# A transformer block on one core: a new order of the first batches, with 16 products whose result nobody reads

## The reference

```python
ada = silu(c) @ W_ada + b_ada            # c: 32 x 288, one row for each batch
shift_msa, scale_msa, gate_msa, shift_mlp, scale_mlp, gate_mlp = split(ada, 6)
h = layernorm(x) * (1 + scale_msa) + shift_msa
x = x + gate_msa * attention(h, W_qkv, b_qkv, W_proj, b_proj)
h = layernorm(x) * (1 + scale_mlp) + shift_mlp
x = x + gate_mlp * (gelu(h @ W_fc1 + b_fc1) @ W_fc2 + b_fc2)
```

## Time and profile before

| | |
|---|---|
| median of 3 runs | 1203.75 us |
| the profiled execution | 1203.89 us, of which the span is 1202.1 us |
| TensorE busy | 1158.4 us (96%), mean granted clock 0.984 |
| VectorE, ScalarE, GpSimd busy | 77%, 71%, 48% |

### The profile page before, as it was taken

The page is one execution under the profiler, slowest core; times in us unless marked ns, Lnnn a source line. Parts: engine busy times, 40 slices in busy tenths (PEclk is TensorE's granted clock), DMA queues, the critical chain, the costliest instruction groups (busy, mean ns, idle before and its releaser), DMA issues.

```text
span 1202.1 us, 28774 instructions
## 1 busy us (share of the span) xinstructions
PE 1158.4 (96%) x10375; PEld 993.9 (83%) x10375; DVE 920.6 (77%) x1928; ACT 858.0 (71%) x1485; POOL 579.2 (48%) x619
## 2 busy tenths in 40 slices
PE   6888999999999999999999999999999999999987
PEld 5666788888888888888888888888888888888777
DVE  5578878878878788887778888877888887877553
ACT  4378777777777777777777787777777777778721
POOL 3012444555544445554454555445455544544664
PEclk9779999999999999999999999999999999999999
DMA  9454554455555445555544555555445555444220
GB/s 276 137 172 156 163 164 147 150 175 168 164 159 163 149 148 173 166 171 164 163 151 151 159 179 165 165 159 167 143 149 181 164 165 161 158 148 156 83 68 20
DMA packets 133814, 186.93 MB, mean 156 GB/s; under 512 B 24284, under 2 KB 102150, under 8 KB 133675
## 3 DMA queue, kind: packets, MB, share of 16 engines
q1 hardware_dynamic: 133513, 184.66, 48.9%
q10 hardware_dynamic: 162, 0.44, 0.1%
HBM read 119.92 MB, written 64.60 MB: 153 GB/s over the span
## 4 chain that ended last, share of the span: by engine, by line
PE 92%; DVE 3%; ACT 2%; DMA 1%; issue 1%; SPq 0%; POOL 0%; ACTq 0%; POOLq 0%; DVEq 0%
PE a_bank L855 13%; PE x_bank L768 12%; PE turn_bank L822 10%; PE b_bank L855 9%; PE score_bank L793 7%; PE st_bank L810 7%; PE b_bank L869 7%; PE b_bank L870 6%; PE b_bank L871 6%; PE a_bank L836 5%; PE x_bank L776 5%; PE x_bank L742 2%; PE a_bank L742 1%; ACT e L942 1%; PE x_bank L745 1%
## 5 line engine op out<-in xcount | busy, mean ns | idle before, releaser
L1128 DVE TENSOR_REDUCE mx<-score_bank 128x2 f32<-128x512 f32 x512 | 332.3, 685 | 94.6 <-PE score_bank L793 92.8
L942 ACT ACTIVATE e<-st_bank 128x1024 f32<-128x1024 f32 x256 | 262.3, 1024 | 163.9 <-PE st_bank L810 163.3
L1285 POOL TENSOR_TENSOR gl<-gl_raw,gh 128x512 fp32r<-128x512 f32 (+1 forms) x160 | 197.2, 1241 | 180.8 <-DVE gh L1193 180.8
L935 ACT CAST ql<-mxt 4x256 fp32r<-4x256 f32 x512 | 205.7, 402 | 5.3
L869 PE MATMUL b_bank<-w,gh 128*128 128x288 f32 x576 | 179.1, 311 | 2.0 <-DVE tmp L1199 1.9
L870 PE MATMUL b_bank<-w,gh 128*128 128x288 f32 x576 | 170.6, 296 | 0.0
L871 PE MATMUL b_bank<-w,gl 128*128 128x288 f32 x576 | 169.6, 295 | 0.0
L822 PE MATMUL turn_bank<-e,ve 128*32 128x256 f32 x2048 | 125.8, 387 | 0.1
L810 PE MATMUL st_bank<-ql,kl 58*128 58x256 f32 x1024 | 117.9, 309 | 6.1 <-ACT e L942 5.0
L793 PE MATMUL score_bank<-kl,ql 58*128 58x256 f32 x1024 | 120.7, 314 | 2.7 <-DVE mx L1128 1.9
L855 PE MATMUL a_bank<-xh,w 128*128 128x256 f32 x640 | 112.2, 298 | 5.5 <-DVE xr L1107 4.0
(11 more groups left out here) (152 smaller groups left out, 2490.9 us busy)
## 6 DMA issues: line engine op xcount, KB each, us to landing
qk_rows<-qst SPq DMA_DIRECT2D x128, 256.0 KB, 3.7
ql<-qk_rows SPq DMA_DIRECT2D x384, 72.0 KB
kl<-qk_rows SPq DMA_DIRECT2D x378, 72.0 KB
o_rows<-on SPq DMA_DIRECT2D x128, 128.0 KB
gate<-gates SPq DMA_DIRECT2D x32, 432.0 KB, 4.5
xin<-in_x SPq DMA_DIRECT2D x32, 288.0 KB, 4.1
x<-in_x SPq DMA_DIRECT2D x32, 288.0 KB, 4.0
out<-x SPq DMA_DIRECT2D x32, 288.0 KB, 2.2
```

What stands on the lines that cost most here:

```text
L935: last = nc.scalar.copy(rows[:, :, :, a, :], src)
L942: nc.scalar.activation(e[:, j % 4, :, :, :].rearrange("p i u l -> p (i u l)"), st_bank[:, :, :, :].rearrange("p i u l -> p (i u l)"), ACT. ...
L1128: nc.vector.tensor_reduce(mx[:, j // HP, i, :, col:col + 1], score_bank[i][:, :].rearrange("p (t l) -> p t l", t=NT), AX.X, ALU.max).then_ ...
L1285: nc.gpsimd.tensor_tensor(gl[:, cols], g[:, cols], gh[:, cols].bitcast(F32), ALU.subtract).then_inc(g_lo, 1)
```

## The change

1. SyncE issues loads 3 to 6 only ahead of its list; 7 to 11 become steps of the list (`("load", 0, 7)` and so on).
2. The second half of the modulation is cut into ten pieces, `("mod", 0, 0)` to `("mod", 0, 9)`, spread over the list. Pieces 0, 1, 5 and 6 have 128 columns of weights and three products each; the other six have 32 columns and three products each.
3. The scores of batches 0 and 1 are made head by head (`s_head`, "sh"): head h waits for the maximum of head h-2 alone.
4. The remainders of loads 3, 4, 6, 7, 9, 10 and 11 are taken by GpSimd (`split_late`) in place of VectorE; loads 5 and 8 stay with VectorE.
5. Twelve steps `("warm", 0, n)` issue n products each, 16 in all, of 128 x 128 weights with 512 columns moving, into `turn_bank`, which nobody reads before it is written anew.
6. The five heads are in a new order; the repeating order and the tails are as before.

```diff
 PE_HEAD = [
-    ("xt", 0, 0), ("xt", 0, 1), ("qk", 0, 0), ("qk", 0, 1), ("qk", 0, 2), ("gate2", 0, 0), ("v", 0, 0), ("v", 0, 1),
-    ("xt", 1, 0), ("mod", 0, 0), ("xt", 1, 1), ("gate2", 0, 1), ("s", 0, 0), ("qk", 1, 0), ("s", 0, 1),
-    ("gate5", 0, 0), ("s", 0, 2), ("qk", 1, 1), ("s", 0, 3), ("gate5", 0, 1), ("qk", 1, 2), ("gate5", 0, 2),
-    ("s", 0, 4), ("gate2", 0, 2), ("v", 1, 0), ("st", 0, 0), ("s", 0, 5), ("v", 1, 1), ("s", 0, 6), ("st", 0, 1),
+    ("xt", 0, 0), ("xt", 0, 1), ("qk", 0, 0), ("qk", 0, 1), ("qk", 0, 2), ("mod", 0, 0), ("v", 0, 0), ("warm", 0, 2),
+    ("gate5", 0, 0), ("v", 0, 1), ("warm", 0, 2), ("gate2", 0, 0), ("xt", 1, 0), ("warm", 0, 2), ("mod", 0, 1), ("mod", 0, 2), ("xt", 1, 1), ("warm", 0, 2),
+    ("gate2", 0, 1), ("gate5", 0, 1), ("qk", 1, 0), ("sh", 0, 0), ("sh", 0, 1), ("warm", 0, 1), ("sh", 0, 2), ("qk", 1, 1),
+    ("sh", 0, 3), ("warm", 0, 1), ("sh", 0, 4), ("mod", 0, 3), ("sh", 0, 5), ("warm", 0, 1), ("mod", 0, 4), ("sh", 0, 6), ("sh", 0, 7), ("warm", 0, 1), ("qk", 1, 2),
+    ("gate5", 0, 2), ("mod", 0, 5), ("mod", 0, 6), ("gate2", 0, 2), ("mod", 0, 7), ("mod", 0, 8), ("mod", 0, 9),
+    ("v", 1, 0), ("sh", 0, 8), ("st", 0, 0), ("sh", 0, 9), ("warm", 0, 1), ("sh", 0, 10), ("v", 1, 1), ("sh", 0, 11), ("warm", 0, 1), ("st", 0, 1),
+    ("sh", 0, 12), ("xt", 2, 0), ("sh", 0, 13), ("warm", 0, 1), ("st", 0, 2), ("sh", 0, 14), ("xt", 2, 1), ("sh", 0, 15), ("warm", 0, 1),
...
 ACT_HEAD = [
-    ("v", 0, 0), ("qkr", 0, 0), ("v", 0, 1), ("qkr", 0, 1), ("qkr", 0, 2), ("qkr", 0, 3), ("qkr", 0, 4),
-    ("round", 0, 2), ("qkr", 0, 5), ("xt", 1, 0), ("xt", 1, 1), ("qk", 1, 0), ("round", 0, 3), ("round", 0, 4),
+    ("qkr", 0, 0), ("round", 0, 1), ("v", 0, 1), ("qkr", 0, 1), ("qkr", 0, 2), ("xt", 1, 0), ("qkr", 0, 3),
+    ("qkr", 0, 4), ("xt", 1, 1), ("qkr", 0, 5), ("round", 0, 2), ("qk", 1, 0), ("round", 0, 3), ("qk", 1, 1),
...
 POOL_HEAD = [
+    ("ln1_stats", 1, 0), ("split", 0, 3), ("split", 0, 4), ("xt", 1, 0), ("ln1_stats", 2, 0), ("xt", 2, 0),
+    ("split", 0, 6), ("ln1_stats", 3, 0), ("split", 0, 7), ("clr", 2, 0), ("clr", 2, 1), ("xt", 3, 0), ("clr", 3, 0),
+    ("split", 0, 9), ("ln1_stats", 4, 0), ("clr", 3, 1), ("split", 0, 10), ("ol", 0, 0), ("proj", 0, 0),
...
 SYNC_HEAD = [
+    ("ln1_stats", 0, 0), ("ln1_stats", 1, 0), ("qkw", 0, 0), ("qkw", 0, 1), ("ln1_stats", 2, 0), ("qkw", 0, 2),
+    ("qkr", 0, 0), ("ln1_stats", 3, 0), ("qkw", 0, 3), ("qkr", 0, 1), ("qkw", 0, 4), ("qkr", 0, 2), ("qkr", 0, 3),
+    ("qkr", 0, 4), ("qkr", 0, 5), ("load", 0, 7), ("load", 0, 8), ("qkr", 0, 12), ("qkr", 0, 13), ("qkr", 0, 14),
...
-            for i in range(N_FIRST, len(loads)):
+            for i in range(N_FIRST, N_EARLY):
                 load_weights(i)
...
+            def warm(_b, n):
+                pe.wait_ge(mod_ready, 1)
+                for _ in range(n):
+                    nc.tensor.matmul(turn_bank[:, :], wq[:, 0, 0:P], wq[:, 0, 0:2 * L], start=True, stop=True)
...
+            def s_head(b, h):
+                j, i = h // 2, h % 2
...
+                wait(pe, s_max[i], PAIRS * b + j)
+                rows = slice(TILE * i, TILE * i + KM)
+                for t in range(NT):
+                    last = nc.tensor.matmul(score_bank[i][:, t * L:(t + 1) * L],
+                                            ql[rows, slot, j % HP, t * P:(t + 1) * P], kl[rows, slot, j % HP, :],
+                                            start=True, stop=True)
+                last.then_inc(s_full[i], 1)
...
+            def split_late(_b, i):
+                _kind, _w, _bias, raw, hi, lo, _n, _k = loads[i]
+                pool.wait_ge(w_hi, i + 1)
+                nc.gpsimd.tensor_tensor(lo, raw, hi.bitcast(F32), ALU.subtract).then_inc(w_late, 1)
```

More of the change, by code:

```diff
@@ L154 @@
-    ("split", 0, 7), ("qk", 4, 1), ("split", 0, 8), ("ln1_apply", 5, 0), ("max", 3, 6), ("max", 3, 7),
[3 rows of a table added]
+    ("max", 0, 3), ("max", 0, 4), ("qk", 1, 1), ("max", 0, 5), ("max", 0, 6), ("max", 0, 7), ("mt", 0, 0),
+    ("ln1_apply", 2, 1), ("qk", 1, 2), ("gates", 0, 0), ("mod", 0, 0), ("max", 0, 8), ("max", 0, 9), ("max", 0, 10),
+    ("max", 0, 11), ("max", 0, 12), ("max", 0, 13), ("max", 0, 14), ("xt", 2, 0), ("max", 0, 15), ("mt", 0, 1),
+    ("xt", 2, 1), ("ln1_stats", 3, 0), ("max", 1, 0), ("max", 1, 1), ("split", 0, 5), ("ln1_apply", 3, 0),
@@ new lines @@
+    ("qkr", 0, 21), ("qkr", 0, 22), ("qkr", 0, 23), ("qkw", 1, 1), ("load", 0, 9), ("load", 0, 10), ("qkw", 1, 2),
+    ("qkw", 1, 3), ("qkr", 1, 0), ("qkr", 1, 1), ("qkr", 1, 2), ("qkr", 1, 3), ("qkr", 1, 4), ("qkr", 1, 5),
+    ("qkw", 1, 4), ("qkr", 1, 6), ("qkr", 1, 7), ("qkr", 1, 8), ("qkr", 1, 9), ("qkr", 1, 10), ("qkr", 1, 11),
+    ("qkr", 1, 12), ("ln1_stats", 4, 0), ("qkr", 1, 13), ("qkr", 1, 14), ("qkr", 1, 15), ("qkr", 1, 16),
+    ("qkr", 1, 17), ("res", 0, 0), ("sr", 0, 0), ("qkr", 1, 18), ("qkr", 1, 19), ("qkr", 1, 20), ("qkr", 1, 21),
@@ new lines @@
+    ("qkr", 1, 22), ("ow", 0, 0), ("qkw", 2, 0), ("qkr", 1, 23), ("ow", 0, 1), ("qkw", 2, 1), ("qkw", 2, 2),
+    ("qkw", 2, 3), ("load", 0, 11), ("or", 0, 0), ("qkw", 2, 4), ("qkr", 2, 0), ("qkr", 2, 1), ("sw", 0, 0),
+    ("qkr", 2, 2), ("qkr", 2, 3), ("qkr", 2, 4), ("qkr", 2, 5), ("qkr", 2, 6), ("qkr", 2, 7), ("qkr", 2, 8),
+    ("ow", 0, 2), ("sr", 0, 1), ("qkr", 2, 9), ("ln1_stats", 5, 0), ("qkr", 2, 10), ("qkr", 2, 11), ("ow", 0, 3),
+    ("rr", 0, 0), ("qkr", 2, 12), ("qkr", 2, 13), ("qkr", 2, 14), ("qkr", 2, 15), ("qkr", 2, 16), ("qkr", 2, 17),
@@ new lines @@
+    ("sw", 0, 1), ("or", 0, 1), ("qkr", 2, 18), ("or", 0, 2), ("qkr", 2, 19), ("qkr", 2, 20), ("qkw", 3, 0),
+    ("qkr", 2, 21), ("rr", 0, 1), ("qkr", 2, 22), ("qkr", 2, 23), ("qkw", 3, 1), ("or", 0, 3), ("sr", 1, 0),
+    ("rr", 0, 2), ("qkw", 3, 2), ("rr", 0, 3), ("or", 0, 4), ("rr", 0, 4), ("or", 0, 5), ("rr", 0, 5), ("ow", 1, 0),
+    ("ow", 1, 1), ("qkr", 3, 0), ("qkw", 3, 3), ("qkr", 3, 1), ("qkw", 3, 4), ("qkr", 3, 2), ("qkr", 3, 3),
+    ("qkr", 3, 4), ("qkr", 3, 5), ("qkr", 3, 6), ("qkr", 3, 7), ("qkr", 3, 8), ("sr", 1, 1), ("qkr", 3, 9),
@@ L187 @@
+    ("qkr", 3, 10), ("ow", 1, 2), ("sw", 1, 0), ("qkr", 3, 11), ("ow", 1, 3), ("qkr", 3, 12), ("qkr", 3, 13),
+    ("or", 1, 0),
 ]
@@ L385, in dit_block @@
         w_split = sem("w_split")
+        w_late = sem("w_late")
         c_loaded = sem("c_loaded")
@@ L686, in _ @@
                 sp.dma_start(minus_p[r0:r0 + nr, 0:1], minus_p[r0:r0 + nr, 1:2]).then_inc(minus_rows, 16)
-            for i in range(N_FIRST, len(loads)):
+            for i in range(N_FIRST, N_EARLY):
                 load_weights(i)
-            run(SYNC_HEAD, SYNC_ORDER, SYNC_TAIL, {"ln1_stats": ln1_stats, "res": res, "qkw": qkw, "qkr": qkr, "ow": ow,
+            run(SYNC_HEAD, SYNC_ORDER, SYNC_TAIL, {"load": lambda _b, i: load_weights(i), "ln1_stats": ln1_stats, "res": res, "qkw": qkw, "qkr": qkr, "ow": ow,
                              "sr": sum_read, "sw": rc_write, "rr": rc_read, "or": o_read, "store": store})
@@ L704, in _, with mod_piece, second_mod @@
             pe.wait_ge(ada_sT, 1)
[L705 to L721 removed]
+            def mod_piece(n, i, c, r):
+                c0 = MOD_OF[2 * n + i] * C
+                cols = slice(c0 + c * P, min(c0 + (c + 1) * P, c0 + C))
+                for k, (_r, nr) in enumerate(K_ROWS):
+                    rows = nr + (k == 2)
+                    to = mod_of[n][:, i, c, :] if c < 2 else mod_of[n][REM * r:REM * (r + 1), i, c, :]
+                    last = nc.tensor.matmul(to, w_ada_sb[k][0:rows, cols], sT[0:rows, k, :],
+                                            start=(k == 0), stop=(k == 2))
+                return last
+            MOD_PIECES = [(i, c, r) for i in range(2) for c in range(3) for r in range(1 if c < 2 else 3)]
+            def mod_columns(n):
+                for i, c, r in MOD_PIECES:
+                    last = mod_piece(n, i, c, r)
+                last.then_inc(ada_mod, 1)
+            def warm(_b, n):
+                pe.wait_ge(mod_ready, 1)
+                for _ in range(n):
+                    nc.tensor.matmul(turn_bank[:, :], wq[:, 0, 0:P], wq[:, 0, 0:2 * L], start=True, stop=True)
+            def second_mod(_b, n):
+                if n == 0:
+                    pe.wait_ge(ada_rest, 16 * 3)
+                last = mod_piece(1, *MOD_PIECES[n])
+                if n == len(MOD_PIECES) - 1:
+                    last.then_inc(ada_mod, 1)
             def gate_rows(v, k):
@@ L797, in s @@
                             last.then_inc(s_full[i], 1)
+            def s_head(b, h):
+                j, i = h // 2, h % 2
+                slot, use = half_use(b, j // HP)
+                if j % HP == 0:
+                    pe.wait_ge(qk_rows[slot], 16 * READS * (use + 1))
+                if b == 0 and h == 0:
+                    pe.wait_ge(consts, FIRST_SET)
+                    pe.wait_ge(kl_chosen, SLOTS)
+                    pe.wait_ge(ql_cleared, 1)
+                wait(pe, s_max[i], PAIRS * b + j)
```

(1 more changed line is left out.)

94 lines of the change are left out of this document (30 added, 64 removed), and 46 rows, old and new, of tables (ACT_HEAD, DVE_HEAD, PE_HEAD, POOL_HEAD).

## The result

| | before | after |
|---|---|---|
| median of 4 runs each | 1203.93 us | 1222.08 us |
| ratio, 95% interval | | 1.014 [1.0119, 1.0161] |
| profiled execution, span | 1203.89, 1202.1 us | 1222.38, 1220.6 us |
| mean granted clock | 0.984 | 0.975 |

The change is slower by 1.4%, 17 us (18.2 by the two medians), where 10 us less were forecast. First the page: busy time by engine, and the granted clock in 40 slices.

The account below looks back on a forecast made before the run. TensorE was full at the upper clock from about 130 us; pauses, waits and low clock bound the head. Cumulative gains of 6.3, 8.9, then 10.6 us, less 0.5 for GpSimd's remainders, gave 1203.9 - 10.1 = 1193.8 us; range 1187 to 1202.

Parts of the forecast that it names:

- Loads later: Ahead of the first score: third q and k write lands at 29.0 instead of 32.1, 3.1 us gained.
- The read lands in "some 2.5 us": Rows read back, last issued about 34.1, land at 36.6; first score at 37.0 instead of 43.31, 6.3 us gained.
- Pieces off the path: Modulation's 7.16 us ahead of the first score is split; seven pieces go behind it, 2.4 us on TensorE at high clock.
- Clock kept from 22 to 60: Head: granted clock 1.00 from 22 to 60 us, where before had stretches at 0.50.
- the clock is not kept: Rival, chance 0.22: clock falls at 32 as before, about 3 us gained at `st(0, 0)`, time 1200.9 us.
- Unread products: Head: 16 cost 4.3 to 7.4 us of TensorE, ten counted as work (2.7), others in waits; could keep the clock high.
- Remainders on GpSimd: Head: VectorE gets back 5.2 us, holds cost 6 (bounds 0 and 11.9); 0.5 us loss taken.
- the rival's 6.7: Slower rival, chance 0.1: GpSimd's remainders hold VectorE behind 55 us, price 11.9 - 5.2 = 6.7 us.
- Behind 72 us: "I carry the 10.6 us": Behind 72 us: order nearly as before, so the 10.6 us gain carries to the end, less 0.5.
- The slower side: Whole kernel: chance 0.08 of a measured time above 1209.8 us.
- does not do what it says: Rival, chance 0.08: gain of the first 70 us given back as batch 1's reads or ScalarE come late; 1203 us.
- an offset at 72 us that is gone at 130: Sign of a wrong forecast: time gained by 72 us is lost again by 130 us.

Follow-up runs that it names:

- d1: After without unread products, pieces ahead of the first score, loops of before, remainders on VectorE: 1211.34 us, 1.0062 to before.
- c2: After with the loops of before, pieces 3 to 9 ahead of the first score, no unread products: 1214.45 us, 1.0055 to before.
- a3: After with only the loop order of the first half of the modulation as before: 1220.28 us, 1.0125 to before.
- a2: After with the last seven modulation pieces ahead of the first score again: 1218.35 us, 1.0104 to before.
- a1: After without its 16 unread products: 1219.76 us, 1.0115 to before.
- b4: Before with only the seven remainders moved to GpSimd: 1213.4 us, 1.0055 to before.
- a4: After with the seven remainders back on VectorE: 1223.82 us, 1.0158 to before.
- b1: Before with only loads 7 to 11 as later steps of SyncE's list: 1206.0 us, 1.0005 to before.
- c1: After with the loops of before, pieces 3 to 9 and 14 unread products alternating ahead of the first score, 22 unread in all: 1216.5 us.
- b3: Before with 16 unread products behind the second v of batch 0, in TensorE's pause: 1203.42 us, 0.9991 to before.
- d2: Before with 8 unread products, one at a time, between the first score and the first pv: 1207.28 us, 1.002 to before.
- d4: d3 plus 2, 4 and 8 unread products ahead of the first score: 1205.93 us, 1.0011 to before.
- b5: Before with late loads, SyncE's last four reads of batch 0 ahead of batch 1's first write, 6 unread products: 1203.65 us, 0.9966 to before.
- d3: b5 without its 6 unread products: 1202.56 us, 0.9977 to before.
- e1: Before with SyncE's whole new list, late loads included, all other lists as before: 1212.7 us, 1.0061 to before.

## Why the prediction was wrong

The parts, by medians and by the ratios (times 1205 us):

| step | us by medians | us by ratios | from |
|---|---|---|---|
| lists, late loads, heads | +6.3 | +7.5 | d1 less before |
| remainders on GpSimd | +3.1 | -0.8 | c2 less d1 |
| loop order of the first half | +1.8 | +1.8 | after less a3 |
| pieces behind the first score | +3.7 | +4.3 | after less a2 |
| unread products | +2.3 | +3.0 | after less a1 |
| sum | +17.2 | +15.8 | measured: 16.9 by the ratio, 18.2 by the medians |

The first two rows lead from before to c2 by construction. What the sum tests is the other three, taken out one at a time (7.8 by medians, 9.1 by ratios) against all at once (after less c2: 7.6 and 10.2). They add up, but for each of them alone the two intervals overlap. The remainders are +6.5 in b4, not told from nothing here and -1.7 in a4. What a term is worth at the end depends on what the later stretches make of it.

1. *Loads later.* The landing is right where the start is not late: 2.85 us in b1 for the 6.93, and in a3 the third write went out at 25.65 (forecast 25.3) and the transposes of batch 1 ran at 30.78 (forecast 30.7). In after it went out at 27.11, and the first read behind it at 31.77 where before had 32.24. Missed was the new loop order of the first half (+2.05 us at the first transposes); the diff has it. The step that turned the landing into 6.3 us of gain at the first score is wrong by itself: see the next point.
2. *The read lands in "some 2.5 us".* This is the step that failed, and the largest error up to the first score. It was argued under the 3.7 us of a write, and no row showed it. It took 8.28 us in b1 and 7.96 in after, with a DMA share of 0.84 at 28 to 39 and at 32 to 45.4 us; in a3 the last of ScalarE's reads left at 33.46, before the forecast 34.1, and the first score came 7.9 us behind it. In before TensorE was busy with 7.16 us of modulation meanwhile, so no wait showed a landing; the last of these reads went out at 34.34 and was used at 43.31, which allows one as long, but does not show it. The first score was forecast at 37.0 and came at 44.12, of which the late start is 2 to 3 us (41.39 in a3) and the landing the rest. In after the last read left at 36.11: in its chain stands SyncE's fetch of x (4.62 us) and the statistics behind it, ahead of the later writes and reads.
3. *Pieces off the path.* The wait for the landing covered them at no cost, and they were moved out of it. Behind the score nothing covers them: +6.2 us there. The forecast priced them in TensorE's list at the upper level and did not ask which wait they would uncover. It took the small ones at 0.2 us each from the earlier trace rows, where three groups run side by side; a piece alone took 0.42 us at the upper level (chain of c1) and 0.59 at the lower, and its seven pieces of 2.4 us took 3.9 at the upper level in c2.
4. *Clock kept from 22 to 60.* It stayed at 1.00 to 44.5 us and then was 0.50 for 41 us. The rival "the clock is not kept" had it fall at 32 and cost 7 us; it fell later and cost more, because all that was put behind the score ran at half pace. TensorE was busy in 38.88 of the 39.6 us behind the fall, with scores, projections, pieces, gates and seven of the unread products, without a rise. Before the fall stood a pause of 4.84 us in after, and only 0.77 and 0.30 us in c1.
5. *Unread products.* Forecast: 2.7 us as work (its two sums hold eight, 2.2 us, and not ten), repaid by the clock. Measured: 6.0 us on the path at the lower level, 2.3 at the end; and in b3, c1, d2 and d4, four other placings, no gain that the intervals show. They do put the fall off: 36.0 in b3 and 32.0 in before, 37.0 in b5 and 33.0 in d3, 46.5 in c1 and 41.5 in c2.
6. *Remainders on GpSimd.* Forecast 0.5, ends 0 and 11.9 for the hold. Alone in before +6.5 us (b4): the rival's 6.7, nearly. Of the rows that showed the hold the full length was the reading, not half, and the chain of after has two such holds. But the experiments on the changed kernel (a4, and d1 against c2) do not show a cost at the end, so what this term is worth in after stays open.
7. *Behind 72 us: "I carry the 10.6 us".* The second stretch was taken as given and cost 4.0 us more (66.9 from `pv` to fc1 where before has 62.8). The new order of SyncE was counted for its first ten steps only; e1 shows that the rest, put alone into before, is worth 7.5 us.

The slower side had 0.08. Its mechanism, GpSimd's hold, is real, but it is one of five terms, and it does not account for the loss. The rival "does not do what it says" (0.08) comes nearest to the first 44 us, though it looked to the reads of batch 1 and it was those of batch 0. Of the milestones named for a wrong forecast the first score after 40 came true; an offset at 72 us that is gone at 130 could not, since at 72 there was a loss and it grew.

Open: what in d1's lists costs the last 6 us, what the remainders cost in after, why the reads take 8 us, why c1 loses 5 us between `pv` and fc1, why the clock falls at 46.5 in c1 behind pauses of under 1 us, and whether b5's six products give anything.

## What to carry to other kernels

A wait that work covers is not in the profile of before: ahead of moving that work, look for the DMA beneath it and take its time from the nearest like transfer in the same traffic, not from a median in quiet. Work without a reader, and small work that was moved "off the path", is to be priced at the lower clock level and at its new place, where something else may stand uncovered. Where an early gain is given back, look at what the in-order DMA queue does next: four reads ahead of two writes turned b1 (1.0005) into d3 (0.9977), and no other part of the change gained anything that shows.
